# Moving three weight corrections from VectorE to GpSimd, and a reordered scatter queue, in a post-norm attention and mixture-of-experts layer

## Chip, cores, metric

The kernel runs on one core of a Trainium2 chip. The engines are TensorE (PE; its weight loads are PEld), VectorE (DVE), ScalarE (ACT), GpSimd (POOL) and SyncE (SP). The metric is device time in microseconds, lower is better.

## The reference

The input x is 2 x 2048 tokens of 256 channels. A linear attention adds a row to each token, a layer norm follows, then a mixture of 8 experts (2 chosen per token, hidden size 192) with a shared gated network, and a second layer norm.

```python
x = _layernorm(x + _L0_attn_ref(x, L0_attn_w_qkv, L0_attn_w_conv1), axis=-1)

def _L0_ffn_ref(x, gate_w, W1, W2, Ws1, Ws2):
    xf = x.reshape(-1, D)
    scores = jax.nn.softmax((xf @ gate_w.T).astype(jnp.float32), axis=-1)
    top_vals, top_idx = jax.lax.top_k(scores, K)
    w_dense = jnp.zeros((T, E), x.dtype).at[jnp.arange(T)[:, None], top_idx].set(weights)
    h = jnp.einsum('td,ehd->teh', xf, W1)
    y, g = jnp.split(h, 2, axis=-1)
    eo = jnp.einsum('teh,edh->ted', y * jax.nn.silu(g), W2)
    z = jnp.einsum('te,ted->td', w_dense, eo)
    z = z + _gated_mlp(xf, Ws1, Ws2)
    return z.reshape(x_shape)

x = _layernorm(x + _L0_ffn_ref(x, ...), axis=-1)
```

## The kernel before

All matmuls of the network run on numbers split into a high part and a low part (hi and lo, fp32r): lo = raw - hi. ACT writes the high parts, DVE or POOL subtracts for the low ones. The weights are split in ten pieces: `high(n)` on ACT (L686), `low(n)` on POOL (L550) for pieces 0 to 6, and `weights_lo(n)` on DVE (L1534) for pieces 7, 8 and 9. From piece 6 on, `low` cuts its work into instructions of 256 columns.

The 4096 tokens are 32 tiles of 128 (one token per partition), in eight groups of four. After the attention, the **group phase** handles groups 0 to 6 in a software pipeline. For each group g, DVE adds the attention row to the tiles (`layer_norm`, two groups ahead), ACT sums squares, POOL makes a rough reciprocal root (`rough_rstd`, L569), DVE refines it by one Newton step (`inverse_std`, one group ahead), ACT writes the normalised rows to x2 (`normalise`), TensorE transposes them (`transposes`), ACT and DVE split them (`rows_hi`, `rows_lo`), TensorE computes the router's logits and the shared network in three chunks of the hidden size (`first_layer`, `second_layer`), with silu on ACT and `product`, `hidden_lo` on DVE and `hidden_hi` on ACT between the layers. DVE picks the two experts of each token (`route`), keeps tables (`tables`) and computes each row's place (`slots`). POOL then scatters the group's rows to `rows_in` in HBM, eight indirect DMAs per group, two for each tile. x2 has two buffers: `normalise(g)` waits for the scatters of group g - 2 and for `add_routed_input` of group g - 2.

The **block phase** (`pairs`, L373) then runs the experts over 71 blocks of 128 rows in pairs, loads the rows from `rows_in`, and scatters the results; the last group's shared network and the second layer norm end it.

Each engine follows its own hand-written order; semaphores tie them. In POOL's loop over groups (L603 to L616) two tiles are scattered, then comes `rough_rstd(q + 2)`, then the other two; in group 6 and 7 a wait stands at that place instead, for the first half of `add_routed_input` of group 6 and for the first expert result. DVE's order in a group is `group(g)` (L1540); its first block is the router, its last `rows_lo` and `add_routed_input`.

## Time and profile before

| | |
|---|---|
| time, median of 3 runs | 334.84 us (333.88 to 335.81) |
| time of the profiled execution | 333.88 us |
| its span, first to last instruction | 332.1 us |
| PE busy | 307.7 us, 93% |
| DVE busy | 264.3 us, 80% |
| POOL busy | 197.2 us, 59% |
| ACT busy | 193.9 us, 58% |

The span is what the timelines count from. Groups 0 to 6 fill it from about 42 to 159 us, the block phase the rest. A row of a timeline gives the start, the duration, the engine, the line, the instruction as out<-in, a count, and in brackets how long the engine was idle before it and what ended that. Two neighbouring rows can overlap a little, since an instruction starts before the one ahead has drained. On PE an instruction's duration is longer than the distance to the next start.

### The profile page before, as it was taken

Reading aid. Unit: us, or ns where it says so; the run is one execution under the profiler, and the core shown is the slowest. Engines: PE = TensorE matmul, PEld = TensorE weight load, DVE = VectorE, ACT = ScalarE, POOL = GpSimd, SP = SyncE. Lnnn points to the kernel's source line nnn. Section 1 sums busy time; section 2 is a strip of 40 time slices with the busy share of each in tenths; the row PEclk is TensorE's granted clock in tenths of the full one; section 3 lists DMA queues with packets and bytes.
Section 4 is the critical chain, followed back from the end, with each engine's and each line's share of the span. In section 5 each row is a group of like instructions: output and inputs, shape, how many; then the busy total and the mean of one; then the engine's idle time right before and its main releaser. Section 6 shows DMA issues by size and latency. Waiting matters only on the chain.

```text
span 332.1 us, 7710 instructions
## 1 busy us (share of the span) xinstructions
PE 307.7 (93%) x2150; PEld 275.7 (83%) x2150; DVE 264.3 (80%) x1089; ACT 193.9 (58%) x440; POOL 197.2 (59%) x229
## 2 busy tenths in 40 slices
PE   3879899999999999999999999999999999999970
PEld 1446678789888889888999999999999999998770
DVE  1796889866888898865899877777799889987685
ACT  1044578846565554646356555666656588688473
POOL 5039580865784638465557544447676866777860
PEclk9979999999999999999999999999999999999977
DMA  6977331121292212442267544448998988976953
GB/s 210 393 270 243 108 92 36 69 100 49 70 254 70 75 42 98 121 147 84 82 200 244 181 131 137 141 125 201 253 211 199 246 203 205 246 214 178 333 193 126
DMA packets 31384, 54.63 MB, mean 164 GB/s; under 512 B 4881, under 2 KB 22545, under 8 KB 31345
## 3 DMA queue, kind: packets, MB, share of 16 engines
q1 hardware_dynamic: 23136, 29.82, 28.9%
q0 software_dynamic: 8208, 24.32, 26.1%
q8 instruction: 20, 0.33, 0.4%
q14 instruction: 20, 0.16, 0.2%
HBM read 29.73 MB, written 24.40 MB: 163 GB/s over the span
## 4 chain that ended last, share of the span: by engine, by line
PE 49%; DVE 18%; POOL 12%; DMA 7%; ACT 6%; issue 6%; SPq 1%; DVEq 0%; ACTq 0%; POOLq 0%
PE bank L1150 20%; PE bank L1184 11%; POOL rows_in L599 8%; PE bank L1116 4%; PE bank L901 4%; DMA rows_in<-x,slot 3%; ACT x L748 3%; DMA x<-rows_out 2%; POOL w1lo L556 2%; DVE mix L1493 2%; PE bank L1164 2%; DVE htlo L1499 2%; PE bank L1057 2%; POOL rough L577 2%; PE bank L1011 2%
## 5 line engine op out<-in xcount | busy, mean ns | idle before, releaser
L668 POOL DMA_INDIRECT rows_out<-stage,place x71 | 69.2, 974 | 46.4 <-ACT stage L847 32.7
L599 POOL DMA_INDIRECT rows_in<-x,slot x64 | 64.6, 1009 | 48.2 <-DVE slot L1405 27.7
L1150 PE MATMUL bank<-w1hi,bx 128*128 x284 | 64.0, 346 | 0.1
L1150 PEld LDWEIGHTS bank<-w1hi,bx 128*128 128x128 f32 x284 | 48.3, 188 | 0.6 <-issue 0.6
L827 ACT ACTIVATE stage<-bank 128x384 f32<-128x384 f32 (+1 forms) x36 | 17.5, 487 | 36.6 <-PE bank L1150 36.5
L847 ACT ACTIVATE stage<-bank,weight 128x256 f32<-128x256 f32 x71 | 30.0, 470 | 10.9 <-PE bank L1184 9.3
L1150 PE MATMUL bank<-w1lo,bx 128*128 x142 | 36.3, 336 | 0.0
L1514 DVE TENSOR_TENSOR bx<-bank,bx 128x512 fp32r<-128x512 f32 (+1 forms) x36 | 24.5, 684 | 13.5 <-ACT bx L768 13.1
L1057 PE MATMUL bank<-ws2hi,hthi 128*128 128x256 f32 x96 | 29.0, 302 | 3.3 <-DVE htlo L1499 3.3
L1033 PE MATMUL bank<-xthi,ws1hi 128*128 128x512 f32 x96 | 31.3, 407 | 0.6 <-DVE mix L1493 0.3
L1033 PE MATMUL bank<-xtlo,ws1hi 128*128 128x512 f32 x96 | 29.9, 393 | 0.0
L1033 PE MATMUL bank<-xthi,ws1lo 128*128 128x512 f32 x96 | 29.8, 392 | 0.0
L764 ACT ACTIVATE hthi<-mix 128x512 fp32r<-128x512 f32 x24 | 15.1, 629 | 23.5 <-DVE mix L1493 23.5
L760 ACT ACTIVATE mix<-bank 128x512 f32<-128x512 f32 x24 | 14.1, 588 | 23.3 <-PE bank L1033 23.2
L1057 PE MATMUL bank<-ws2hi,htlo 128*128 128x256 f32 x96 | 27.5, 286 | 0.0
L1057 PE MATMUL bank<-ws2lo,hthi 128*128 128x256 f32 x96 | 27.5, 286 | 0.0
L1150 PEld LDWEIGHTS bank<-w1lo,bx 128*128 128x128 f32 x142 | 25.7, 188 | 0.0
L1220 DVE CUSTOM_DVE_ANT_0 junk<-xs,bank 128x256 f32<-128x256 f32 x64 | 22.8, 415 | 3.2 <-DMA xs<-x 2.9
L1057 PEld LDWEIGHTS bank<-ws2hi,hthi 128*128 128x128 f32 x96 | 18.8, 196 | 5.7 <-issue 2.9
L1184 PE MATMUL bank<-w2hi,hthi 128*128 x71 | 22.8, 321 | 0.0
L1499 DVE TENSOR_TENSOR htlo<-mix,hthi 128x512 fp32r<-128x512 f32 x24 | 17.2, 716 | 6.7 <-ACT hthi L764 6.6
L768 ACT ACTIVATE bx<-bank 128x512 fp32r<-128x512 f32 (+1 forms) x36 | 21.2, 591 | 2.0 <-PE bank L1116 2.0
(255 smaller groups left out, 856.8 us busy)
## 6 DMA issues: line engine op xcount, KB each, us to landing
stage<-rows_in SPq DMA_DIRECT2D x71, 133.0 KB, 2.7
xs<-rows_out POOLq DMA_DIRECT2D x12, 512.0 KB, 6.1
xs<-x SPq DMA_DIRECT2D x8, 512.0 KB, 8.1
out<-xs SPq DMA_DIRECT2D x7, 512.0 KB, 5.3
stage<-w_t SPq DMA_DIRECT2D x8, 384.0 KB, 4.1
rows_in<-clear SPq DMA_DIRECT2D x16, 133.0 KB, 4.0
rows_out<-stage,place POOLq DMA_INDIRECT x71
stage<-w_t SPq DMA_DIRECT2D x2, 512.0 KB, 3.9
```

The costliest lines, as they stand in the source:

```text
L599: pool.indirect_dma_start(rows_in[0:E * CAP, :], bass.IndirectOffsetOnAxis(slot[:, q * G + t, k:k + 1], 0), x2[q % 2][:, t, :], None).then ...
L668: pool.indirect_dma_start(rows_out[:, :], bass.IndirectOffsetOnAxis(place[:, 2 * j + b:2 * j + b + 1], 0), by[j % 4][:, b * C:(b + 1) * C] ...
L768: act.activation(bxhi[j % 2][:, 0:C * width(j)], bank_x[j % 2][:, 0:C * width(j)], ACT.Copy).then_inc(s_bxhi, 1)
L827: act.activation(bsg[j % 2][:, 0:width(j)], bank_h[j % 2][:, 0:width(j), H:F], ACT.Silu).then_inc(s_bsg, 1)
L847: ins = act.activation(by[j % 4][:, b * C:(b + 1) * C], result(j, b), ACT.Copy, scale=weight[:, j // 2 % 2, at_w:at_w + 1])
L1033: mm = pe.matmul(bank[:], w[:, k, o:o + P], xt[:, k, :], start=(a == 0), stop=(a == len(steps) - 1))
L1057: mm = pe.matmul(bank[:, (t % 2) * C:(t % 2 + 1) * C], ht[:, m, t * P:(t + 1) * P], w[:, m, :], start=(t % 2 == 0 and n == 0 and a == 0), ...
L1150: mm = pe.matmul(bank_h[j % 2][:, b, 0:F], bx[j % 2][:, (2 * b + k) * P:(2 * b + k + 1) * P], w[:, bass.ds(e, 1), k, :], start=(a == 0), s ...
L1184: mm = pe.matmul(result(j, b), ht, w[:, bass.ds(e, 1), :], start=(a == 0), stop=(a == len(steps) - 1))
L1220: vec.tensor_tensor_reduce(junk[:, nth % 2, :], xs[:, tile, :], row, 1.0, 0.0, ALU.mult, ALU.add, dst[:, b, t:t + 1]).then_inc(s_dot, 1)
L1499: vec.tensor_tensor(htlo[:, c, :], prod[buf(g, m)], hthi[:, c, :].bitcast(F32), ALU.subtract).then_inc(s_ht, 1)
L1514: vec.tensor_tensor(bxlo[j % 2][:, at], bank_x[j % 2][:, at], bxhi[j % 2][:, at].bitcast(F32), ALU.subtract).then_inc(s_bx, 1)
```

## The change

POOL's loop over groups issues the eight scatters of a group in one row, with `rough_rstd(q + 2)` in their middle for groups 1 to 5 only; `rough_rstd(2)` follows the eight scatters of group 0. The two waits in groups 6 and 7 are dropped. After the scatters of groups 1 to 4 POOL does `low(6)` to `low(9)`; `weights_lo` is gone from DVE. On DVE in group 0, `token_shift(1)` and two tiles of `layer_norm(2)` come ahead of `rows_lo(1)`, the other two tiles behind it.

```diff
@@ POOL @@
-            def scatter(q, t):
-                for k in range(K):
-                    pool.indirect_dma_start(
...
             for q in range(NG):
                 pool.wait_ge(s_slot, q + 1)
-                for t in range(2):
-                    scatter(q, t)
-                if q < NG - 2:
-                    rough_rstd(q + 2)
-                elif q < LAST:
-                    pool.wait_ge(s_zev[0], q + 1)
-                else:
-                    pool.wait_ge(s_byev, results_signalled(1))
-                for t in range(2, G):
-                    scatter(q, t)
-                if q == 1:
-                    low(6)
+                for t in range(G):
+                    if t == 2 and 0 < q < NG - 2:
+                        rough_rstd(q + 2)
+                    for k in range(K):
+                        pool.indirect_dma_start(
...
+                if q == 0:
+                    rough_rstd(2)
+                elif q < 5:
+                    low(5 + q)
@@ DVE @@
-            def weights_lo(n):
-                vec.wait_ge(s_whi, n + 1)
-                vec.wait_ge(s_wlo, n)
-                vec.tensor_tensor(LO[n], RAW[n], HI[n].bitcast(F32), ALU.subtract).then_inc(s_wlo, 1)
-
             def group(g):
...
-                if 3 <= g <= 5:
-                    weights_lo(4 + g)
...
                 if g == 0:
                     hidden_lo(0, 2)
-                    rows_lo(1)
                     token_shift(1)
-                    layer_norm(after, range(G))
+                    layer_norm(after, range(0, 2))
                 if g > 1 and after < NG:
                     layer_norm(after, range(2, G))
                 if g:
                     hidden_lo(g, 2)
-                    rows_lo(g + 1)
+                rows_lo(g + 1)
+                if g == 0:
+                    layer_norm(after, range(2, G))
```

In the lists below, rough is the rough reciprocal root, vareps its input, rows_in the scattered rows, x_0 and x_1 the two buffers of normalised rows. POOL at group 0, before:

```order
L577 TENSOR_TENSOR rough<-vareps,half 128x4 [waits ln1_var_eps]
L599 DMA rows_in<-x_0,slot 33792x266 [waits slots,ln1_rstd]
L599 DMA rows_in<-x_0,slot 33792x266 x3
L575 TENSOR_SCALAR vareps<-square 128x4 [waits ln1_squares]
L577 TENSOR_TENSOR rough<-vareps,half 128x4 [waits ln1_var_eps]
L599 DMA rows_in<-x_0,slot 33792x266 x4
```

and now:

```order
L577 TENSOR_TENSOR rough<-vareps,half 128x4 [waits ln1_var_eps]
L602 DMA rows_in<-x_0,slot 33792x266 [waits slots,ln1_rstd]
L602 DMA rows_in<-x_0,slot 33792x266 x7
L575 TENSOR_SCALAR vareps<-square 128x4 [waits ln1_squares]
L577 TENSOR_TENSOR rough<-vareps,half 128x4 [waits ln1_var_eps]
L602 DMA rows_in<-x_1,slot 33792x266 [waits slots]
```

The rough root of group 2 has moved from behind four scatters to behind eight.

POOL from the end of group 2 to the start of group 4, before (w2lo and w2rlo are pieces 7 and 8):

```order
L599 DMA rows_in<-x_0,slot 33792x266 x4
L599 DMA rows_in<-x_1,slot 33792x266 [waits slots]
L599 DMA rows_in<-x_1,slot 33792x266 x3
L575 TENSOR_SCALAR vareps<-square 128x4 [waits ln1_squares]
L577 TENSOR_TENSOR rough<-vareps,half 128x4 [waits ln1_var_eps]
L599 DMA rows_in<-x_1,slot 33792x266 x4
L599 DMA rows_in<-x_0,slot 33792x266 [waits slots]
```

and now:

```order
L602 DMA rows_in<-x_0,slot 33792x266 x4
L556 TENSOR_TENSOR w2lo<-stage,w2hi 128x256 [waits weights_hi]
L556 TENSOR_TENSOR w2lo<-stage,w2hi 128x256 x3
L602 DMA rows_in<-x_1,slot 33792x266 [waits slots]
L602 DMA rows_in<-x_1,slot 33792x266 x3
L575 TENSOR_SCALAR vareps<-square 128x4 [waits ln1_squares]
L577 TENSOR_TENSOR rough<-vareps,half 128x4 [waits ln1_var_eps]
L602 DMA rows_in<-x_1,slot 33792x266 x4
L556 TENSOR_TENSOR w2rlo<-stage,w2rhi 128x256 [waits weights_hi]
L556 TENSOR_TENSOR w2rlo<-stage,w2rhi 128x256 x3
L602 DMA rows_in<-x_0,slot 33792x266 [waits slots]
```

Four pieces of a correction stand between the scatters of one group and the next.

DVE at the end of group 0, before (xtlo is `rows_lo`, small is `token_shift`, xs,rowsum is `layer_norm`, xs<-bank,x is `add_routed_input`):

```order
L1499 TENSOR_TENSOR htlo<-mix,hthi 128x512 [waits hidden_hi]
L1360 TENSOR_TENSOR xtlo<-bank,xthi 128x512 [waits x2t_hi] x2
L1262 COPY small<-bank 128x1 [waits att1_tensor]
L1280 SCALAR_TENSOR_TENSOR xs,rowsum<-row,tok,xs 128x256 x4
L1508 TENSOR_TENSOR xs<-bank,x_0 128x512 [waits shared_psum0]
L1508 TENSOR_TENSOR xs<-bank,x_0 128x512 [waits shared_psum1]
```

and now:

```order
L1491 TENSOR_TENSOR htlo<-mix,hthi 128x512 [waits hidden_hi]
L1254 COPY small<-bank 128x1 [waits att1_tensor]
L1272 SCALAR_TENSOR_TENSOR xs,rowsum<-row,tok,xs 128x256 x2
L1352 TENSOR_TENSOR xtlo<-bank,xthi 128x512 [waits x2t_hi] x2
L1272 SCALAR_TENSOR_TENSOR xs,rowsum<-row,tok,xs 128x256 x2
L1500 TENSOR_TENSOR xs<-bank,x_0 128x512 [waits shared_psum0]
L1500 TENSOR_TENSOR xs<-bank,x_0 128x512 [waits shared_psum1]
```

`rows_lo` has moved behind the small copy and two of the four tiles.

DVE in group 4 between the tables and the slots, before (mix is `product`, rn to minus is `inverse_std`, htlo is `hidden_lo`):

```order
L1471 SCALAR_TENSOR_TENSOR ends<-taken,ends 128x8 [waits table_steps]
L1538 TENSOR_TENSOR w2rlo<-stage,w2rhi 128x1024 [waits weights_lo,weights_hi,table_steps]
L1493 TENSOR_TENSOR mix<-bank,mix 128x512 [waits silu]
L1287 TENSOR_TENSOR rn<-rough 128x4 [waits ln1_newton0]
L1289 TENSOR_TENSOR rn<-vareps,rn 128x4 [waits ln1_newton1]
L1291 TENSOR_SCALAR rn<-rn 128x4 [waits ln1_newton2]
L1293 TENSOR_TENSOR rstd<-rough,rn 128x4 [waits ln1_newton3]
L1295 TENSOR_TENSOR minus<-nmean,rstd 128x4 [waits ln1_rstd]
L1499 TENSOR_TENSOR htlo<-mix,hthi 128x512 [waits hidden_hi]
L1493 TENSOR_TENSOR mix<-bank,mix 128x512 [waits silu]
L1280 SCALAR_TENSOR_TENSOR xs,rowsum<-att,tok,xs 128x256 x2
L1393 TENSOR_TENSOR slotf<-bank,begin 128x32 [waits positions]
```

and now:

```order
L1463 SCALAR_TENSOR_TENSOR ends<-taken,ends 128x8 [waits table_steps]
L1485 TENSOR_TENSOR mix<-bank,mix 128x512 [waits silu,table_steps]
L1279 TENSOR_TENSOR rn<-rough 128x4 [waits ln1_newton0]
L1281 TENSOR_TENSOR rn<-vareps,rn 128x4 [waits ln1_newton1]
L1283 TENSOR_SCALAR rn<-rn 128x4 [waits ln1_newton2]
L1285 TENSOR_TENSOR rstd<-rough,rn 128x4 [waits ln1_newton3]
L1287 TENSOR_TENSOR minus<-nmean,rstd 128x4 [waits ln1_rstd]
L1491 TENSOR_TENSOR htlo<-mix,hthi 128x512 [waits hidden_hi]
L1485 TENSOR_TENSOR mix<-bank,mix 128x512 [waits silu]
L1272 SCALAR_TENSOR_TENSOR xs,rowsum<-att,tok,xs 128x256 x2
L1385 TENSOR_TENSOR slotf<-bank,begin 128x32 [waits positions]
```

The correction of 1024 columns ahead of the product is gone, and the rest is as it was.

## Rows read from the trace of the kernel before

**Rows 1.** The page's costliest groups: busy, mean ns | idle before, releaser
```profile
L599 POOL DMA_INDIRECT rows_in<-x,slot x64 | 64.6, 1009 | 48.2 <-DVE slot L1405 27.7
```

**Rows 2.** Table of stretches: us, busy by engine, clock, DMA share, GB/s
```profile
105.00:122.00 17.00, 16.37 (x108) 14.20 (x106) 14.28 (x64) 9.30 (x24) 9.10 (x10) 1.00 0.18 65
...
sum 48.00, PE 47.01 PEld 41.13 DVE 41.72 ACT 25.67 POOL 27.94; mean PE 15.67 PEld 13.71 DVE 13.91 ACT 8.56 POOL 9.31
```

**Rows 3.** Timeline of PE: start, us, instruction, count [idle before, releaser]
```profile
60.84 0.71 PE L1033 MATMUL bank<-xthi,ws1hi 128*128 128x512 f32 x2 [0.18 <-DVE xs L1508]
...
73.85 1.09 PE L999 MATMUL bank<-ident,x 128*128 128x128 f32 x8
...
119.01 0.73 PE L1033 MATMUL bank<-xthi,ws1hi 128*128 128x512 f32 x2 [0.27 <-DVE mix L1493]
...
141.54 0.38 PE L1057 MATMUL bank<-ws2hi,hthi 128*128 128x256 f32 x1 [0.35 <-DVE htlo L1499]
```

**Rows 4.** Timeline of POOL, scatters of group 0
```profile
58.92 2.01 POOL L599 DMA_INDIRECT rows_in<-x,slot  x1 [0.30 <-issue]
...
62.50 0.96 POOL L599 DMA_INDIRECT rows_in<-x,slot  x1 [0.30 <-issue]
...
65.20 1.06 POOL L599 DMA_INDIRECT rows_in<-x,slot  x1 [0.20 <-issue]
...
69.10 0.96 POOL L599 DMA_INDIRECT rows_in<-x,slot  x1 [0.30 <-issue]
```

**Rows 5.** Timeline of DVE, groups 0 and 1
```profile
57.14 1.27 DVE L1360 TENSOR_TENSOR xtlo<-bank,xthi 128x512 fp32r<-128x512 f32 x2
...
66.51 0.15 DVE L1287 TENSOR_TENSOR rn<-rough 128x4 f32<-128x4 f32 x1
...
67.10 0.16 DVE L1293 TENSOR_TENSOR rstd<-rough,rn 128x4 f32<-128x4 f32 x1
...
69.56 0.69 DVE L1493 TENSOR_TENSOR mix<-bank,mix 128x512 f32<-128x512 f32 x1 [0.86 <-ACT mix L760]
```

**Rows 6.** Timeline of ACT, groups 1 and 5
```profile
70.29 0.63 ACT L764 ACTIVATE hthi<-mix 128x512 fp32r<-128x512 f32 x1 [0.76 <-DVE mix L1493]
71.72 2.08 ACT L748 ACTIVATE x<-xs,minus,rstd 128x256 f32<-128x256 f32 x4 [0.80 <-DMA rows_in<-x,slot]
...
136.15 2.08 ACT L748 ACTIVATE x<-xs,minus,rstd 128x256 f32<-128x256 f32 x4 [0.71 <-issue]
```

**Rows 7.** Line 1538, the corrections on DVE: ns min/median/max, first and last start
```profile
L1538 DVE TENSOR_TENSOR w2rlo<-stage,w2rhi x2: 1225/1250/1276, 117.1 to 132.5; 128x1024 fp32r<-128x1024 f32 x2
```

**Rows 8.** Timeline of POOL and DVE, group 2, around POOL's low(6)
```profile
85.11 0.63 DVE L1293 TENSOR_TENSOR rstd<-rough,rn 128x4 f32<-128x4 f32 x1
...
85.61 3.35 POOL L556 TENSOR_TENSOR w2lo<-stage,w2hi 128x256 fp32r<-128x256 f32 x4
...
85.78 0.66 DVE L1295 TENSOR_TENSOR minus<-nmean,rstd 128x4 f32<-128x4 f32 x1
...
86.36 1.31 DVE L1499 TENSOR_TENSOR htlo<-mix,hthi 128x512 fp32r<-128x512 f32 x1
...
88.19 1.06 DVE L1280 SCALAR_TENSOR_TENSOR xs<-att,tok,xs 128x256 f32<-128x256 f32 x1
...
89.18 0.47 DVE L1280 SCALAR_TENSOR_TENSOR xs<-att,tok,xs 128x256 f32<-128x256 f32 x1
```

**Rows 9.** Line 1499, htlo on DVE: ns min/median/max, first and last start
```profile
L1499 DVE TENSOR_TENSOR htlo<-mix,hthi x24: 659/690/1306, 51.3 to 320.2; 128x512 fp32r<-128x512 f32 x24
```

**Rows 10.** Timeline of POOL, scatters of groups 3 and 4
```profile
111.69 0.19 POOL L575 TENSOR_SCALAR vareps<-square 128x4 f32<-128x4 f32 x1 [1.04 <-ACT squares L723]
...
122.85 1.30 POOL L599 DMA_INDIRECT rows_in<-x,slot  x1 [4.79 <-DVE slot L1405]
...
133.57 0.96 POOL L599 DMA_INDIRECT rows_in<-x,slot  x1 [0.30 <-issue]
```

**Rows 11.** Timeline of POOL, scatters of groups 6 and 7
```profile
159.44 0.96 POOL L599 DMA_INDIRECT rows_in<-x,slot  x1 [1.83 <-DVE xs L1508]
...
173.26 0.96 POOL L599 DMA_INDIRECT rows_in<-x,slot  x1 [2.88 <-ACT stage L847]
```

More of the change, by code:

```diff
@@ L594, in _ @@
             pool.wait_ge(s_rs, 4)
-            def scatter(q, t):
-                for k in range(K):
-                    pool.indirect_dma_start(
-                        rows_in[0:E * CAP, :], bass.IndirectOffsetOnAxis(slot[:, q * G + t, k:k + 1], 0),
-                        x2[q % 2][:, t, :], None).then_inc(s_sc[q % 2], 16)
             for q in range(NG):
                 pool.wait_ge(s_slot, q + 1)
-                for t in range(2):
-                    scatter(q, t)
-                if q < NG - 2:
-                    rough_rstd(q + 2)
-                elif q < LAST:
-                    pool.wait_ge(s_zev[0], q + 1)
-                else:
-                    pool.wait_ge(s_byev, results_signalled(1))
-                for t in range(2, G):
-                    scatter(q, t)
-                if q == 1:
-                    low(6)
+                for t in range(G):
[3 more added lines that the diff above has]
+                        pool.indirect_dma_start(
+                            rows_in[0:E * CAP, :], bass.IndirectOffsetOnAxis(slot[:, q * G + t, k:k + 1], 0),
+                            x2[q % 2][:, t, :], None).then_inc(s_sc[q % 2], 16)
+                if q == 0:
+                    rough_rstd(2)
+                elif q < 5:
+                    low(5 + q)
             results = rows_out[0:DUMMY].rearrange("(k b p j) c -> k b p j c", k=K, b=B, p=P)
```

## The prediction

> **What bounds the kernel now.** I read the page's costliest groups first, then the table of stretches, then TensorE's own timeline for its waits, and last the timelines of POOL, DVE and ACT beside it. On the page POOL's scatters stand high, with 27.7 us of idling for DVE's slots ahead of them [rows 1]: POOL is waited for, but has room. In the group phase, where all the edits lie, TensorE is busy 47.01 of 48 us and DVE 41.72 [rows 2]. So the groups are TensorE's work laid end to end, and DVE, ACT and POOL matter only where a TensorE instruction waits for them. The reader should see in [rows 3] how small those waits are: 0.18 us for xs at the start of group 1, 0.27 us for the product in group 4, 0.35 us for htlo in group 5. What the edits can win there is no more than these waits. A delay has no such cap: an engine that is late by more than its slack pushes TensorE, and TensorE never catches up.
>
> **The change, part by part.** Durations are of one execution, whose time was 333.88 us (span 332.1, so 1.8 around it); the median of the three runs is 334.84, and I add the sum to the median.
>
> **1. rough_rstd(2) goes behind all eight scatters of group 0.** Before, it stands in the middle: a scatter ends at 62.50 + 0.96 = 63.46, the next one starts at 65.20, where otherwise 0.30 us lie between two, so the step costs the scatters 1.44 us. rough was ready at 65.00, the 0.20 before 65.20, and so 1.54 after that scatter. The last scatter ends at 69.10 + 0.96 = 70.06 [rows 4]. Now it ends at 70.06 - 1.44 = 68.62, and rough is ready not at 65.00 but at 68.62 + 1.54 = 70.16. Who waits? inverse_std(2) on DVE, which read rough at 66.51 with no wait [rows 5]: it now stands still 3.65 us. Queued behind it are value_row(1), two tiles of layer_norm(3), product(1, 1) and slots(1). From 66.51 to the start of DVE's idle 0.86 us before product(1, 1), that is to 68.70, is 2.19 us of work [rows 5], so the product starts at 70.16 + 2.19 = 72.35 instead of 69.56, 2.79 us late. ACT converts it (hthi, at 70.29 before, 0.73 after the product) and normalises group 2 behind that: at 72.35 + 0.73 + 0.53 = 73.61 instead of 71.72 [rows 6]. Until now ACT sat idle for 0.80 us before 71.72, for the scatters of group 0 to free the buffer; they are done 1.44 us sooner, which is the gain the move can have, but DVE is now later than they are. TensorE's transposes of group 2 started at 73.85, right behind the last of the four tiles [rows 3, 6]: they start **1.9 us later**, and everything after hangs on them. slots(1) is late too, 2.8 us, but the second half of those scatters waits for ACT's squares of group 3, which are 1.9 late as well.
>
> **2. rows_lo(1) goes behind two tiles of layer_norm(2).** It ran from 57.14 to 58.41 [rows 5], just before TensorE's logits of group 1. Two tiles at 0.47 at most [rows 8] and some 0.3 of waiting for TensorE's maximum (estimated from the order: it is issued behind second-layer matmuls) put its end at about 59.6, so the logits start 0.8 us late; the first-layer matmuls behind them waited for xs anyway, so 0.5 us is left at 60.84 [rows 3]. This delay lies inside the 1.9 us of part 1: with TensorE 0.5 us later, the chain through rough is still what ends last. It costs nothing by itself; if that cover were gone, it would cost 0.5.
>
> **3. Three corrections (w2lo, w2rlo) go from DVE to POOL.** DVE gives up 1.25 us in each of groups 3, 4 and 5 [rows 7]. POOL takes each as four pieces, behind the scatters of groups 2, 3 and 4. The one such set that POOL already does shows the price: four pieces in 3.35 us. POOL has that room: ahead of the scatters of group 4 it idled 4.79 us [rows 10], and 27.7 us over the eight groups [rows 1]. But DVE is slowed during it: rstd 0.63 where it took 0.16 in group 1 [rows 5], minus 0.66 for as short a step, htlo 1.31 where the median is 0.69, xs 1.06 where 0.47 [rows 8, 9], together 0.47 + 0.50 + 0.62 + 0.59 = 2.2 us. So DVE gives up 1.2 and may get back up to 2.2, and later in the group, right ahead of slots. The Trainium skill (SBUF — State Buffer, "two separate sides") says that DVE and GpSimd share a pair of ports under an exclusive lock, held for a whole instruction, and that a DVE instruction with two SBUF inputs is blocked by it. The rows agree: all four slowed ones read two tensors in SBUF. By that rule the move can lose on DVE what it was to gain.
> In groups 3 and 5 none of it reaches TensorE: the scatters that follow have 1.04 us of waiting for squares in their middle (one of two such rows in [rows 10]), and 0.7 us (three blocked instructions and a later start, less 1.2) fits in it. In group 4 two things happen. The product in front of which DVE did the correction comes 1.2 us sooner, and TensorE's wait of 0.27 goes. And slots(4) moves by -1.20 + (0.47 + 0.50 + 0.62) = +0.39, three of the four blocked instructions lying ahead of it. Its scatters run with no wait inside, 122.85 to the last start at 133.57 [rows 10], and normalise(6) on ACT starts 2.58 us after that, at 136.15 [rows 6]; behind it stands htlo, for which TensorE already waits 0.35 [rows 3]. So 0.39 goes through. The sum of group 4 is -0.27 + 0.39 = **+0.1**; its bounds are -0.27 - 0.35 = -0.6 with no slowing (more than the wait can't be won) and -0.27 + 0.98 = +0.7 with all four in front. I take +0.1, since the set in group 2 shows the slowing.
> The last correction is now ready behind the scatters of group 4, at 133.57 + 0.96 + 3.35 = 138; it is needed only by the blocks after group 6, whose xs was not ready before 159.4 [rows 11], so its place is free.
>
> **4. The waits of POOL in groups 6 and 7 go.** They cost POOL 1.83 and 2.88 us [rows 11]. Nobody waits for those scatters: there is no group 8 to normalise, and the rows they write are loaded for pair 8 and later. TensorE has no wait for POOL there. I take 0; against it stands only that the writes of group 7 now meet the loads of the first blocks' rows: +0.3 at most.
>
> The sum: 1.9 + 0 + 0.1 + 0 = **+2.0 us**, so 334.84 + 2.0 = **336.8 us**; the span would be 334.1.
>
> **The rivals.**
> **A: the second scatter gets shorter.** It took 2.01 us, where others take 0.96 [rows 4]; beside it four tiles of layer_norm, each at most 0.47, ran back to back on DVE from the end of rows_lo(1) at 58.4 to about 60. The change puts rows_lo, which reads PSUM, between them. If they were what held it, it takes some 1.05 now, and all of part 1 comes 0.95 earlier: +1.05, **335.9**. For it: the coincidence. Against it: tiles run beside the scatters of every group, and the longest of those later ones took 1.30 [rows 10]; the second may have been slow because it was one of the first. The same page of the Trainium skill names a trap in which DVE keeps GpSimd from writing its descriptors; it gives it for another kind of DVE instruction, so I leave this the smaller chance.
> **B: the slowing reaches TensorE in every group.** Then groups 3, 4 and 5 each pay 2.2 - 1.2 = 1.0 less the 0.27: +1.9 + 2.7 = +4.6 at worst, about half of it with the slack of 1.04 counted: +3.3, **338.1**. It decides from where a blocked instruction stands ahead of a TensorE wait with less slack than the block.
> **C: faster.** DVE, not TensorE, sets the pace of groups 3 to 5 (41.72 of 48 us busy), so the 3 x 1.25 = 3.75 us given up there come back in full and pay for part 1: 1.9 - 3.75 = -1.9, **333.0**. It decides once more than 3.6 of them reach TensorE. Against it: TensorE's waits there add up to under 1 us.
> **D: part 1 is covered.** TensorE does the second layer's first part before the transposes, and if POOL's rough is ready early enough (A) and group 4 wins its waits (-0.6), +0.3 is left: **335.1**, no change that can be told.
>
> **How the numbers follow.** Chances: forecast 0.52, A 0.17, B 0.12, C 0.07, D 0.12. A measurement of this kernel tells about 0.5% (1.7 us) from no change. The forecast lies 0.3 above that line; with its own spread (1.3 to 2.6) three quarters of it is over, so slower is 0.39 + 0.12 + a little of A = 0.53, faster 0.07, the rest 0.40. The range leaves out C and the worst of B: from 334.8 (D with 0.3 less) to 338.3 (B with 0.2 more).
>
> **What would show it.** Right: DVE idle for some 3.6 us ahead of rn in group 1 with POOL's rough as releaser; the transposes of group 2 near 75.8; DVE instructions over 0.6 us beside POOL's w2lo and w2rlo pieces in groups 3 to 5; the wait of 0.27 at 119 gone; the pairs of blocks at their present pace, the whole tail only shifted. Wrong: rough of group 2 ready by 68 (POOL faster than I think), a TensorE wait for a product or for htlo above 1 us in groups 3 to 5 (B), or slots that come earlier than before from group 4 on, in spite of a late group 2 (C).

## The result, and the profile after

The changed kernel took 337.4 us in the median of 20 runs, where the kernel before, run beside it, took 335.65: a ratio of 1.007 (95% interval 1.0051 to 1.009), or 2.35 us more. That is past the 0.5% that can be told, on the slower side, and inside the range; the forecast was +2.0. The profiled execution of the changed kernel took 340.0 us (span 338.3), among its slowest, while that of before (333.88) was among the fastest of its own. Their difference of 6.1 us is therefore more than the change, and durations of single steps are compared, not the two spans. One execution each of the kernel before, of e1 (350 us) and of e12 (517 us) ran at a low clock throughout (mean 0.84, 0.85 and 0.56), and the ratios and intervals below leave such executions out.

First the page of the changed kernel: busy time of each engine, the granted TensorE clock in 40 slices of the span (tenths of full speed), and the scatters with the idle time ahead of them.

```profile
PE 311.8 (92%) x2150; PEld 276.7 (82%) x2150; DVE 267.1 (79%) x1086; ACT 194.1 (57%) x440; POOL 204.7 (61%) x241
...
PEclk9959999699999999999999999999999999999996
...
L602 POOL DMA_INDIRECT rows_in<-x,slot x64 | 64.2, 1003 | 46.3 <-DVE slot L1397 29.7
```

The scatters are as before, with two us less of idling in all (46.3 against 48.2 in [rows 1]). New is the 6 in the eighth slice of PEclk, which is 59 to 68 us.

TensorE's timeline of the changed kernel; this answers [rows 3].

```profile
61.01 0.36 PE L1003 MATMUL bank<-gate,xthi 128*128 128x16 f32 x2 [0.77 <-DVE xtlo L1352]
...
63.30 1.20 PE L1025 MATMUL bank<-xthi,ws1hi 128*128 128x512 f32 x2
64.29 1.05 PE L1025 MATMUL bank<-xtlo,ws1hi 128*128 128x512 f32 x2
65.15 1.05 PE L1025 MATMUL bank<-xthi,ws1lo 128*128 128x512 f32 x2
...
78.63 0.60 PE L991 MATMUL bank<-ident,x 128*128 128x128 f32 x4
...
94.00 0.35 PE L1049 MATMUL bank<-ws2hi,hthi 128*128 128x256 f32 x1 [0.45 <-DVE mix L1485]
...
127.56 0.36 PE L1049 MATMUL bank<-ws2hi,hthi 128*128 128x256 f32 x1 [0.93 <-DVE mix L1485]
```

Three things differ. TensorE pauses for 0.77 us ahead of the logits of group 1, because rows_lo(1) now comes behind two tiles. Soon after, its pairs of first-layer matmuls start 0.86 us apart (64.29 to 65.15), where in the other trace they are about 0.46 apart. And in group 4 there is a wait of 0.93 us for a product, which before had no counterpart (the 0.27 us at 119.01 in [rows 3] is gone). The table of stretches of the changed kernel shows why the pairs are slow: us, busy time by engine, granted clock, DMA share and GB/s.

```profile
60.00:62.00 2.00, 1.23 (x12) 1.06 (x11) 2.00 (x7) 1.84 (x5) 1.52 (x2) 1.00 0.35 128
62.00:64.00 2.00, 2.00 (x11) 1.90 (x11) 1.24 (x5) 2.00 (x9) 1.46 (x2) 0.56 0.23 81
64.00:66.00 2.00, 2.00 (x6) 1.52 (x5) 1.85 (x20) 0.96 (x2) 1.62 (x2) 0.50 0.41 142
66.00:68.00 2.00, 2.00 (x6) 1.61 (x5) 0.38 (x2) 0.00 (x0) 1.39 (x3) 0.50 0.20 70
68.00:70.00 2.00, 2.00 (x26) 0.75 (x29) 0.57 (x1) 0.60 (x1) 1.84 (x3) 0.73 0.42 136
```

Behind the pause the granted clock was 0.50, the lower of TensorE's two levels (1.2 GHz), from about 62 to 69 us; from 62 to 70 us the mean is 0.57, so 8 x 0.43 = 3.4 us of full-speed work were lost. TensorE is "busy" all the time there, so the waits don't show it. This execution is not typical: its mean granted clock over the span is 0.970, where the median of the 45 recorded executions of the changed kernel is 0.981. The six of them at 0.973 or less took 338.8 to 340.1 us, the eight at 0.985 or more 335.3 to 337.4. The Trainium skill (TensorE: Matmul & The Clock Gate, "The HAM clock gate") has these two levels and says that idling brings the lower; here the level did fall behind a pause.

Now POOL, DVE and ACT of the changed kernel, for [rows 4] to [rows 6].

```profile
60.17 0.97 POOL L602 DMA_INDIRECT rows_in<-x,slot  x1 [0.31 <-issue]
...
67.86 0.96 POOL L602 DMA_INDIRECT rows_in<-x,slot  x1 [0.30 <-issue]
...
69.17 1.04 POOL L577 TENSOR_TENSOR rough<-vareps,half 128x4 f32<-128x4 f32 x1
...
69.43 0.69 DVE L1485 TENSOR_TENSOR mix<-bank,mix 128x512 f32<-128x512 f32 x1 [3.05 <-ACT mix L752]
...
71.42 0.15 DVE L1279 TENSOR_TENSOR rn<-rough 128x4 f32<-128x4 f32 x1
```

The eight scatters ran back to back, the second in 0.97 us instead of 2.01, and rough came at 70.21. DVE then read it at 71.42 without a wait. Its long idle stands earlier, 3.05 us ahead of product(1, 0): the late and slow TensorE had moved the wait to another place. The pause of 0.77 us is the only idle time of TensorE in this trace between 58 and 84 us.

Last, the price of POOL's pieces, for [rows 8]: POOL, DVE and ACT in groups 3 and 4 of the changed kernel.

```profile
107.25 2.84 POOL L556 TENSOR_TENSOR w2lo<-stage,w2hi 128x256 fp32r<-128x256 f32 x4
...
107.69 0.69 DVE L1485 TENSOR_TENSOR mix<-bank,mix 128x512 f32<-128x512 f32 x1 [0.43 <-ACT mix L752]
...
108.30 2.08 DVE L1272 SCALAR_TENSOR_TENSOR xs<-att,tok,xs 128x256 f32<-128x256 f32 x1
...
123.42 2.83 POOL L556 TENSOR_TENSOR w2rlo<-stage,w2rhi 128x256 fp32r<-128x256 f32 x4
...
122.89 0.66 DVE L1281 TENSOR_TENSOR rn<-vareps,rn 128x4 f32<-128x4 f32 x1
123.58 0.66 DVE L1283 TENSOR_SCALAR rn<-rn 128x4 f32<-128x4 f32 x1
124.28 0.65 DVE L1285 TENSOR_TENSOR rstd<-rough,rn 128x4 f32<-128x4 f32 x1
124.97 0.67 DVE L1287 TENSOR_TENSOR minus<-nmean,rstd 128x4 f32<-128x4 f32 x1
125.55 1.25 DVE L1491 TENSOR_TENSOR htlo<-mix,hthi 128x512 fp32r<-128x512 f32 x1
...
125.67 2.08 ACT L740 ACTIVATE x<-xs,minus,rstd 128x256 f32<-128x256 f32 x4 [1.73 <-DVE minus L1287]
```

In group 4 the pieces met the whole chain rn, rstd, minus: four steps of 0.16 us took 0.66 each, +2.0 us, and htlo another 0.6. (The first of the four, at 122.89, ended 0.13 us after the first piece began and stood beside the last scatter before that, so its 0.5 may belong to the scatter; in e3 it is the same.) ACT idled 1.73 us for minus. In group 3 they met one tile of layer_norm, which took 2.08 instead of 0.47.

### The profile page after: what moved, and what is told of

Its sections match the earlier page's. It is cut to its first block, busy times and chain, and to the rows that moved or that the text cites. A ratio compares the mean times of both kernels' runs of the same rounds, so it can differ in the third digit from the quotient of the medians.

```text
span 338.3 us, 7718 instructions
## 1 busy us (share of the span) xinstructions
PE 311.8 (92%) x2150; PEld 276.7 (82%) x2150; DVE 267.1 (79%) x1086; ACT 194.1 (57%) x440; POOL 204.7 (61%) x241
## 4 chain that ended last, share of the span: by engine, by line
PE 62%; DVE 22%; DMA 4%; issue 4%; ACT 4%; POOL 2%; SPq 1%; DVEq 0%; ACTq 0%
PE bank L1142 19%; PE bank L1176 10%; PE bank L1025 10%; PE bank L1049 4%; PE bank L1108 4%; PE bank L1003 4%; DVE xs L1272 3%; PE bank L893 3%; DVE htlo L1491 2%; DVE mix L1485 2%; DMA x<-rows_out 2%; POOL rows_in L602 2%; PE bank L1156 2%; PE bank L905 2%; DMA xs<-x 2%
## 5 line engine op out<-in xcount | busy, mean ns | idle before, releaser
L660 POOL DMA_INDIRECT rows_out<-stage,place x71 | 69.3, 977 | 48.0 <-ACT stage L839 34.2
L602 POOL DMA_INDIRECT rows_in<-x,slot x64 | 64.2, 1003 | 46.3 <-DVE slot L1397 29.7
L1025 PE MATMUL bank<-xthi,ws1hi 128*128 128x512 f32 x96 | 32.2, 417 | 0.2 <-ACT xthi L748 0.2
L1025 PE MATMUL bank<-xtlo,ws1hi 128*128 128x512 f32 x96 | 30.8, 403 | 0.0
L1025 PE MATMUL bank<-xthi,ws1lo 128*128 128x512 f32 x96 | 30.7, 401 | 0.0
L1049 PE MATMUL bank<-ws2lo,hthi 128*128 128x256 f32 x96 | 26.8, 279 | 0.0
L1049 PE MATMUL bank<-ws2hi,htlo 128*128 128x256 f32 x96 | 26.7, 279 | 0.0
L1049 PEld LDWEIGHTS bank<-ws2hi,hthi 128*128 128x128 f32 x96 | 18.1, 188 | 8.9 <-DVE htlo L1491 6.1
L1485 DVE TENSOR_TENSOR mix<-bank,mix 128x512 f32<-128x512 f32 x24 | 16.5, 686 | 8.6 <-ACT mix L752 8.5
```

The lines of the kernel that those rows point to most:

```text
L602: pool.indirect_dma_start(rows_in[0:E * CAP, :], bass.IndirectOffsetOnAxis(slot[:, q * G + t, k:k + 1], 0), x2[q % 2][:, t, :], None).then ...
L660: pool.indirect_dma_start(rows_out[:, :], bass.IndirectOffsetOnAxis(place[:, 2 * j + b:2 * j + b + 1], 0), by[j % 4][:, b * C:(b + 1) * C] ...
L1025: mm = pe.matmul(bank[:], w[:, k, o:o + P], xt[:, k, :], start=(a == 0), stop=(a == len(steps) - 1))
L1049: mm = pe.matmul(bank[:, (t % 2) * C:(t % 2 + 1) * C], ht[:, m, t * P:(t + 1) * P], w[:, m, :], start=(t % 2 == 0 and n == 0 and a == 0), ...
L1485: vec.tensor_tensor(prod[buf(g, m)], hidden_banks(g, m)[0][:], sg[buf(g, m)], ALU.mult).then_inc(s_pr, 1)
```

## The experiments

Two yardsticks are used. One is the time, measured beside the kernel before. The other is a span inside one profiled execution, from the start of the logits of one group to that of a later one; it leaves out how late the head of the kernel came. Starts are those of each kernel's first gate matmuls in the timeline of TensorE.

| kernel (us) | logits 0 to 1 | 1 to 2 | 0 to 2 | 4 to 5 | 5 to 6 | 2 to 7 |
|---|---|---|---|---|---|---|
| before | 15.15 | 19.66 | 34.81 | 16.30 | 16.02 | 81.46 |
| e4_waits | 15.15 | 19.54 | 34.69 | 16.17 | 17.84 | 83.19 |
| e1_rough | 15.14 | 21.39 | 36.53 | 16.15 | 17.82 | 83.09 |
| e2_rowslo | 16.10 | 19.09 | 35.19 | 16.17 | 17.81 | 83.34 |
| e11 (reorder again) | 16.10 | 18.97 | 35.07 | 16.19 | 17.83 | 83.64 |
| e3_lows | 15.16 | 19.56 | 34.72 | 17.36 | 16.30 | 83.38 |
| e5 (all but the reorder) | 15.14 | 21.40 | 36.54 | 17.46 | 16.19 | 83.40 |
| changed kernel | 16.10 | 22.09 | 38.19 | 17.38 | 16.19 | 83.36 |
| e9 (changed kernel again) | 16.08 | 21.09 | 37.17 | 17.36 | 16.37 | 83.71 |
| e10 (changed kernel, pause filled) | 16.00 | 22.11 | 38.11 | 17.34 | 16.28 | 83.32 |

The experiments e5 to e8 ran on a second chip and e9 to e12 on a third, where the kernel before took 348.7 and 346.8 us instead of 335.2. Ratios are only compared within a chip.

### One part alone: e1 to e4

**e1_rough**, only the move of rough_rstd(2):

```diff
-                if q < NG - 2:
+                if 0 < q < NG - 2:
                     rough_rstd(q + 2)
...
                 for t in range(2, G):
                     scatter(q, t)
+                if q == 0:
+                    rough_rstd(2)
```

> The kernel before with one edit: rough_rstd(2) stands behind all eight scatters of group 0. Theory P (the prediction, part 1): DVE stands still some 3.6 us ahead of rn in group 1, the transposes of group 2 start 1.9 us later (75.8 against 73.85 in the profile before), time +1.9 us. Theory Q (the trace of after, where rough came 68.6 to 70.2 and DVE had no wait for it, because TensorE itself was late): if the second scatter takes 0.97 again, rough is ready near 69 and the cost is about +1.0 us; it is hidden only if something else has delayed group 1.

It took 336.73 us (12 runs), ratio 1.0038 (1.0006 to 1.007), about +1.3. POOL, DVE and TensorE of e1_rough:

```profile
68.63 1.04 POOL L577 TENSOR_TENSOR rough<-vareps,half 128x4 f32<-128x4 f32 x1
...
69.70 0.16 DVE L1289 TENSOR_TENSOR rn<-rough 128x4 f32<-128x4 f32 x1 [3.54 <-POOL rough L577]
...
72.61 0.36 PE L1059 MATMUL bank<-ws2hi,hthi 128*128 128x256 f32 x1 [0.72 <-DVE mix L1495]
...
75.16 1.09 PE L1001 MATMUL bank<-ident,x 128*128 128x128 f32 x8 [0.94 <-ACT x L750]
```

That is the predicted mechanism to the tenth: DVE idle 3.54 us for rough (3.65 predicted), and TensorE waits 0.72 and 0.94 us. From the first layer at 60.40 to the transposes at 75.16 are 14.76 us, where [rows 3] give 13.01: +1.75, against +1.9 predicted. The table has +1.7 in group 1 and nothing in groups 0 and 4; the 17.82 in group 5 is explained under e4.

**e2_rowslo**, only the reorder around rows_lo(1):

```diff
-                    rows_lo(1)
                     token_shift(1)
-                    layer_norm(after, range(G))
+                    layer_norm(after, range(0, 2))
...
-                    rows_lo(g + 1)
+                rows_lo(g + 1)
+                if g == 0:
+                    layer_norm(after, range(2, G))
```

> The kernel before with one edit: rows_lo(1) stands behind token_shift(1) and two tiles of layer_norm(2). Theory P: TensorE's logits of group 1 start 0.8 us later, 0.5 us is left at the first layer, time +0.5 us. Theory R (the trace of after): the idle of 0.77 us ahead of the logits is followed by a stretch at the lower clock (granted 0.50 from 62.3 to 69), which costs over 3 us in that stretch: time +1.5 to +4 us, and the same dip in the profile of this run. If P holds the granted clock stays at 1.00 there.

It took 337.63 us (9 runs), ratio 1.0082 (1.0049 to 1.0116), about +2.7, as much as the whole change. Yet its profiled execution shows little. Its TensorE and POOL, then its table of stretches:

```profile
61.42 0.36 PE L1011 MATMUL bank<-gate,xthi 128*128 128x16 f32 x2 [0.77 <-DVE xtlo L1360]
...
60.55 0.97 POOL L599 DMA_INDIRECT rows_in<-x,slot  x1 [0.31 <-issue]
```

```profile
62.00:64.00 2.00, 2.00 (x17) 1.86 (x17) 1.75 (x9) 1.85 (x8) 1.70 (x2) 1.00 0.39 140
64.00:66.00 2.00, 2.00 (x10) 1.49 (x8) 1.86 (x18) 1.38 (x3) 1.41 (x3) 1.00 0.22 76
```

The pause of 0.77 us is there, the clock behind it is full this time, and the table gives +0.4 from logits 0 to 2: 0.95 lost in group 0, 0.5 won back in group 1. The other executions differ by their mean granted clock over the span: 0.979 in the median, against 0.985 for the kernel before. 0.006 of 335 us is 2 us of full-speed work. Its four executions at 0.983 or more took 336.0 to 337.4 us, its five at 0.979 or less 337.6 to 339.6. That pointed to the clock behind the pause, in some executions but not in the profiled one. It is not shown: the mean also covers the head (16 to 32 us) and the end (from 316 us on), where every trace of this chip has the lower level and loses 6.1 to 7.6 us in all, and no trace of this kernel has it behind the pause. It also shows that the second scatter is short (0.97) because of the reorder: in e1, e3 and e4, which leave the order alone, it took 2.01.

**e3_lows**, only the corrections moved to POOL:

```diff
-                if q == 1:
-                    low(6)
+                if 1 <= q <= 4:
+                    low(5 + q)
...
-                if 3 <= g <= 5:
-                    weights_lo(4 + g)
```

> The kernel before with one edit: pieces 7, 8 and 9 of the weight corrections on POOL behind the scatters of groups 2, 3 and 4, and not on DVE. Theory P: +0.1 us, TensorE's wait of 0.27 at group 4 gone, slots(4) 0.4 later. Theory B (slowing reaches TensorE): +1 to +3 us, with a TensorE wait of 0.9 in group 4 for the product, as the trace of after shows. Theory C (DVE was the pace): up to -3.7 us.

It took 335.67 us (12 runs), ratio 1.0026 (0.9999 to 1.0053), about +0.9. TensorE and ACT of e3_lows in group 4:

```profile
121.80 2.08 ACT L748 ACTIVATE x<-xs,minus,rstd 128x256 f32<-128x256 f32 x4 [1.70 <-DVE minus L1295]
...
123.70 0.36 PE L1057 MATMUL bank<-ws2hi,hthi 128*128 128x256 f32 x1 [0.92 <-DVE mix L1493]
```

The same two waits as in the changed kernel, without its other parts. Group 4 is 1.1 us longer in every kernel with this part (17.34 to 17.50) than in the others (16.15 to 16.60).

**e4_waits**, only the waits of POOL in groups 6 and 7 dropped:

```diff
                     rough_rstd(q + 2)
-                elif q < LAST:
-                    pool.wait_ge(s_zev[0], q + 1)
-                else:
-                    pool.wait_ge(s_byev, results_signalled(1))
```

> The kernel before with one edit: POOL's two waits in groups 6 and 7 are dropped. Theory P: 0 us, at most +0.3. Theory W (the waits kept descriptor work of POOL away from DVE and the loads at the start of the block phase): +0.5 us or more, with TensorE waits between 165 and 182 that the profile before does not have.

It took 334.88 us (12 runs), ratio 0.9996 (0.9964 to 1.0028): nothing, as predicted. It taught something else. Its group 5 took 17.84 us where before has 16.02, although the edit comes later in the program. ACT's normalise there:

```profile
138.75 2.07 ACT L744 ACTIVATE x<-xs,minus,rstd 128x256 f32<-128x256 f32 x4 [2.70 <-issue]
```

The idle of 2.70 was 0.71 in [rows 6]. Five traces have this late normalise (e1, e2, e4, e11, e12), and none of those with the corrections on POOL. What goes with it, without exception, is a race between DVE's correction w2rlo (the third of those that the change takes away) and one scatter of group 4. First DVE and POOL of e4, then of e7, which has the correction on DVE too:

```profile
133.08 1.23 DVE L1534 TENSOR_TENSOR w2rlo<-stage,w2rhi 128x1024 fp32r<-128x1024 f32 x1
...
133.28 1.86 POOL L599 DMA_INDIRECT rows_in<-x,slot  x1 [0.30 <-issue]
```

```profile
134.75 1.22 DVE L1541 TENSOR_TENSOR w2rlo<-stage,w2rhi 128x1024 fp32r<-128x1024 f32 x1
...
134.59 0.96 POOL L599 DMA_INDIRECT rows_in<-x,slot  x1 [0.30 <-issue]
```

In e4 DVE started 0.20 us ahead of the scatter, and the scatter took 1.86. In e7 the scatter started 0.16 ahead of DVE and took 0.96. So it is in all eight traces with this correction on DVE: DVE first by 0.20 or 0.21 in e1, e2, e4, e11 and e12 and the scatter 1.85 to 1.87 us long; the scatter first by 0.15 or 0.16 in before, e7 and e8 and 0.96 long. In the five, group 5 takes 17.81 to 17.84 us, 1.5 to 1.8 more than before's 16.02 or the 16.22 and 16.34 of e7 and e8. The delay has two halves. Counted from the logits of group 5, the last scatter of group 4 starts 0.9 to 1.0 us later, and from its start to the normalise it is 3.3 us, where the three that won the race have 2.6 to 2.9; why it lands later is not settled. The corrections on POOL end this race. They cost 1.1 us in group 4 each time and save up to 1.7 in group 5 in those executions that lose it; that this is why e3 pays only 0.9 in all is argued and not shown, since how often the kernel before loses the race was not measured. The trace of before was one that won it, so the prediction could not see a gain there.

The four parts measured +1.3, +2.7, +0.9 and -0.1, together +4.8, against +2.35 (1.7 to 3.0) for the whole. Each part is known to about 1 us and their sum to about 2, so that the parts overlap is likely and not certain. The next runs asked where.

### The pause and the clock: e5 to e8

**e5_after_old_rows**, the changed kernel with the old order around rows_lo(1):

```diff
+                    rows_lo(1)
                     token_shift(1)
-                    layer_norm(after, range(0, 2))
+                    layer_norm(after, range(G))
...
-                rows_lo(g + 1)
-                if g == 0:
-                    layer_norm(after, range(2, G))
+                    rows_lo(g + 1)
```

> The changed kernel with rows_lo(1) put back ahead of token_shift(1) and the whole of layer_norm(2): parts 1, 3 and 4 of the change without part 2. Theory A (costs add up): rough_rstd(2) alone measured +1.3 us and the low pieces +0.9 us, so this gives about +2.2 us, 337.4, as much as the whole change, with VectorE idle some 3 us ahead of rn in group 1 and the transposes of group 2 about 1.7 us later after the first layer than in before. Theory B (the reorder is the dear part, because TensorE's 0.8 us pause ahead of the logits of group 1 is followed in many executions by a granted clock of 0.5, while the wait of part 1 is then hidden): the time lies below that of the changed kernel only if A's two costs are smaller than what the reorder costs; the mean granted clock over the span returns to about 0.985 from the changed kernel's 0.981, and no slice between 60 and 70 us is granted less than 1.00.

352.42 us (6 runs), ratio 1.0104 (1.007 to 1.0138), +3.6 on this chip, more than e1 and e3 together on the first (+2.2). The clock was 1.00 from 60 to 80 us, and DVE's wait for rough is back:

```profile
71.46 0.16 DVE L1279 TENSOR_TENSOR rn<-rough 128x4 f32<-128x4 f32 x1 [3.55 <-POOL rough L577]
```

Up to the logits of group 7 the costs add as Theory A says (36.54 and 17.46 in the table are e1's and e3's numbers). The rest of the +3.6 lies behind group 7: from those logits to the last matmul it took 177.8 us, and 173.7 in e7 and e8 on the same chip. On the first chip the changed kernel took 162.2 there and the kernel before 162.7.

**e6_after_filled**, the changed kernel with work in the pause:

```diff
                     pe.wait_ge(s_slot, g)
+                if g == 1:
+                    for _ in range(14):
+                        pe.matmul(banks[2][:, 256:384], onesb[:], onesb[:], start=True, stop=True)
                 pe.wait_ge(s_xt, g + 1)
```

> The changed kernel with 14 more matmuls of 128 columns (bf16 ones into an unused part of bank 2) between TensorE's two waits ahead of the logits of group 1, about 0.8 us of work where it paused for 0.77 us. They are not part of the computation. Theory B (the pause itself is cheap, the clock behind it is dear): the granted clock stays 1.00 from 60 to 72 us, the mean clock goes from 0.981 to about 0.985 and the time falls by 1 to 1.5 us, to 336.0 to 336.4; the wait of part 1 then shows itself again. Theory A (contention and waits alone, the clock plays no part): the extra matmuls change nothing or cost up to 0.5 us, 337.4 to 337.9.

**e7_reorder_filled**, e2 with the same addition:

> The kernel before with the reorder alone (rows_lo(1) behind two of the four tiles of layer_norm(2)) and the same 14 matmuls in TensorE's pause ahead of the logits of group 1. The reorder alone measured +2.7 us. Theory B (clock): most of this goes, +0.8 or less is left, which is what the late low parts of the rows take from TensorE: 335.2 to 336.0, mean clock 0.985. Theory A (the order on VectorE makes work late by itself): +2.7 us stays, 337.9, and the mean clock says nothing.

**e8_head_filled**, the kernel before with such matmuls in the head:

```diff
+            pe.wait_ge(s_set, 1)
+            warm(6, banks[6])
             channel_logits(0)
+            warm(18, banks[6])
             token_column(0)
+            warm(8, banks[6])
             token_row(0)
```

(and six more inside channel_logits(0).)

> The kernel before with 38 matmuls of 128 columns (bf16 ones into bank 6, before its first use) in four pauses of TensorE between 13.5 and 19.5 us (0.52, 0.52, 1.44 and 0.58 us long in the trace of before); they are not part of the computation. In every profile so far the granted clock is about 0.5 for 3 to 4 us somewhere between 20 and 32 us. Theory B (a pause brings it): with the pauses filled the clock stays 1.00 there, TensorE wins up to 1.5 us of the head, and as much as the head's later waits let through reaches the end, 0 to -1.5 us: 333.7 to 335.2. Theory C (it comes with the rise of work at 20 us, whatever the pauses were): the low clock stays, and the time is that of before or up to 0.3 us more.

e6 took 355.33 us (6 runs), ratio 1.0207 (1.0167 to 1.0247); e7 348.59 (12 runs), 1.0001 (0.9972 to 1.0029); e8 349.25 (12 runs), 1.0009 (0.9979 to 1.0039). e7 fits Theory B, e6 speaks against it, and neither had its unfilled partner on that chip; e9 to e12 mend this. e8 is a miss. Its clock was full where before had the low level (0.57 from 20 to 24 us), but it fell later, behind the next pause. Its table of stretches, and below it one line of e2's:

```profile
20.00:24.00 4.00, 4.00 (x60) 2.87 (x59) 3.79 (x23) 2.32 (x3) 1.65 (x1) 1.00 0.80 271
24.00:28.00 4.00, 2.60 (x37) 2.01 (x35) 3.83 (x24) 1.48 (x1) 4.00 (x4) 1.00 0.27 78
28.00:32.00 4.00, 3.98 (x41) 1.77 (x38) 1.09 (x7) 1.99 (x4) 3.77 (x3) 0.58 0.95 316
```

```profile
28.00:32.00 4.00, 4.00 (x43) 2.01 (x40) 1.17 (x7) 1.99 (x4) 3.71 (x3) 0.57 0.93 316
```

The shift can't be put down to the filling. e2 and e11, whose head is that of the kernel before, also have the clock at 1.00 from 20 to 28 us and at 0.57 from 28 to 32; the other eleven traces have the low level between 16 and 26. So the place of this stretch changes between executions of the same head.

### Filled and unfilled on one chip: e9 to e12

e9 is the changed kernel, e10 is e6, e11 is e2 and e12 is e7, word for word.

> The changed kernel itself, beside its filled version on one chip. It was 0.7% slower than before (interval 1.0051 to 1.009) where the kernel before takes 335.6 us. The chip of the last four experiments took 348.7 us for the kernel before and had a 3 us wait at the routing of the last group that no trace of the first chip shows, so ratios of the two chips are not to be mixed. Both theories: 1.005 to 1.009 on a chip like the first; on one like the second Theory A (low pieces and first-scatter wait add up: e5 measured 1.0104 there without the reorder) gives 1.010 to 1.015.

> The changed kernel with 14 extra matmuls in TensorE's pause ahead of the logits of group 1, now beside the changed kernel on the same chip. Theory B (the low clock behind the pause is what the reorder costs): the clock is 1.00 from 60 to 72 us, and the kernel is 1 to 1.5 us faster than e9. Theory A' (with the clock full, TensorE only meets the late rn of part 1 sooner and waits there, as a 1.7 us pause between 66 and 72 us in the second chip's trace suggests): within 0.5 us of e9.

> The kernel before with the reorder alone, beside its filled version on one chip. It measured 1.0082 (1.0049 to 1.0116) on the first chip, with a mean clock of 0.979 against 0.985. Both theories: 1.005 to 1.011 again on a chip like the first. If it is 1.002 or less, the +2.7 us of the first measurement was an accident of its nine runs and the reorder is cheap, as the prediction had it.

> The reorder alone with the 14 extra matmuls in the pause. It measured 1.0001 (0.9972 to 1.0029) on the second chip, where the unfilled version was not run. Theory B: 1.0 to 1.002, thus 1.5 to 2.5 us faster than e11, with a mean clock 0.004 to 0.006 higher. Theory A (late work on VectorE, no part for the clock): equal to e11 within 0.5 us.

| kernel | median us (runs) | ratio to before | 95% interval | median clock |
|---|---|---|---|---|
| e9, changed kernel | 353.23 (6) | 1.0177 | 1.0135 to 1.0218 | 0.970 |
| e10, the same, filled | 352.64 (6) | 1.0179 | 1.0143 to 1.0216 | 0.974 |
| e11, reorder alone | 348.04 (12) | 1.0039 | 1.0002 to 1.0076 | 0.976 |
| e12, the same, filled | 347.12 (12) | 1.0019 | 0.9989 to 1.0049 | 0.978 |

With the pause filled the clock stayed at 1.00 from 60 to 72 us in all four traces, but the changed kernel is not faster: e9 and e10 are equal in time, as Theory A' had it, though not for its reason (below). In the reorder alone filling gains 0.9 us of the 1.4; the intervals overlap, and it is less than the 1.5 to 2.5 that was expected, so this has the sign of Theory B and doesn't prove it. Two more expectations missed: e9's 1.0177 lies above both bands, and e11's 1.0039 below its own. The tables of stretches of e9 (first two lines) and of e10 (last two), and below them what TensorE and ACT of e10 did:

```profile
64.00:66.00 2.00, 2.00 (x6) 1.60 (x5) 1.69 (x14) 0.79 (x1) 1.70 (x2) 0.50 0.42 144
66.00:68.00 2.00, 2.00 (x19) 0.92 (x22) 0.14 (x1) 0.60 (x1) 1.39 (x3) 0.73 0.23 83
```

```profile
64.00:66.00 2.00, 2.00 (x25) 1.14 (x27) 1.85 (x18) 0.21 (x1) 1.39 (x3) 1.00 0.22 76
66.00:68.00 2.00, 0.99 (x13) 0.44 (x6) 0.51 (x4) 0.00 (x0) 1.70 (x2) 1.00 0.41 136
```

```profile
64.90 2.00 PE L893 MATMUL bank<-xs,stage 128*32 128x256 f32 x27
67.90 0.43 PE L893 MATMUL bank<-xs,stage 128*32 128x256 f32 x2 [1.00 <-issue]
...
69.37 0.60 ACT L752 ACTIVATE mix<-bank 128x512 f32<-128x512 f32 x1 [5.17 <-remote]
```

e9 has the low clock again behind its pause. e10 has none, but both TensorE and ACT stood still until 69.3 us for reasons that the profile doesn't name: TensorE in the middle of 32 matmuls between which the program has no wait. e6, on another chip, has the same stop at the same place (0.19, 0.34 and 0.99 us, and 5.30 for ACT). e7 has none from 60 to 72 us, nor has e12, though TensorE's program is the same; what differs there is POOL, which in e6 and e10 issues its eight scatters without a step between them. That alone doesn't bring the stop either: POOL does the same in the changed kernel, e9 and e5, where TensorE stands still without a named reason for at most 0.50 us from 60 to 72 us. So in e10's trace filling removed one loss and another stood in its place. What stopped the two engines stays open.

Behind group 7 the slower chips differ in two more ways. e9's TensorE at the routing of the last group, and a stretch of its table:

```profile
172.92 0.21 PE L1034 MATMUL bank<-chosen,trib 128*128 128x40 bf16 x1 [3.18 <-DVE chosen L1379]
```

```profile
188.00:190.00 2.00, 1.69 (x8) 1.73 (x9) 1.80 (x11) 1.62 (x4) 0.96 (x1) 0.50 0.73 181
```

The wait for DVE is 3.0 to 3.4 us long in all four traces of the changed kernel and its variants there (e5, e6, e9, e10) and in e7, and absent in e8, e11, e12 and on the first chip. The low clock comes between 168 and 194 us in all eight traces of e5 to e12, costs 1.7 to 5.1 us of full-speed work, and comes in none of the first chip. It takes 3.4 us more in e5 than in e8 and 1.7 more than in e7, a good part of the 4.1 us by which e5 is longer behind group 7. No run changed either of the two alone.

## Why the prediction was right, point by point

- **What bounds the kernel.** Right: where TensorE's idle or its clock differs, the span differs; DVE's and POOL's own totals don't tell it.
- **1, rough_rstd(2), +1.9.** Right, and shown alone: +1.75 in e1's trace, +1.7 in group 1 in e1 and e5, +1.3 (0.2 to 2.3) in time. In the changed kernel the wait itself is not seen: rough was ready at 70.21 and read at 71.42, because TensorE was late already. So of the signs that the prediction named, its first one (DVE idle 3.6 us for rough) is absent there, and the transposes of group 2 came at 78.63 us and not near 75.8, of which 1.2 is a later head.
- **2, rows_lo(1), 0 under the cover of part 1.** This step failed. The 0.8 of late logits was right (0.93 to 0.95 in the traces with the reorder, 0.84 to 0.87 with the pause filled), and so was the 0.5 left without cover (+0.4 from logits 0 to 2). But the cover did not hold: with both parts (the changed kernel, e6, e9, e10), logits 0 to 2 took 37.17 to 38.41, which is 2.4 to 3.6 more than before's 34.81 and not 1.9. In the changed kernel's trace it was the other way round, the lost clock hid the wait of part 1; in e6 and e10 the unexplained stop stood there. And the price of a pause was taken to be its length. Behind it the granted clock fell to 0.50, for some 7 and 3 us, in both traces of the changed kernel (there and in e9), in neither trace of the reorder alone (e2, e11), and in none of the ten traces without the pause was it under 1.00 from 60 to 72 us. By those rows a pause of 0.77 us cost 3.4 us more in one execution and 1.7 in another (e9, from 62 to 68 us). In the median it was less: the mean clock is 0.981 against 0.985 for the kernel before (beside e1 to e4), 1.3 us of full-speed work, wherever in the span it was lost.
- **3, the corrections, +0.1.** The contention was right and mis-sized. The prediction took three blocked instructions and their effect on slots; it was the chain rn, rstd, minus with htlo behind it, 2.0 + 0.6 us, and it reached TensorE by way of ACT's normalise and the product (waits of 0.92 in e3, 0.93 in the changed kernel). Group 4 paid 1.1, above the bound of +0.7. What the step left out altogether is the gain in group 5, up to 1.7, of a scatter that no correction of DVE can meet. In time the part cost +0.9 (0 to 1.8).
- **4, the dropped waits, 0.** Right (e4).
- **The rivals.** A's premise was true: the second scatter takes 0.97 once the order changes, shown by e2. Its price of -0.95 did not come, since that scatter was no longer what ended last. B was true in one group out of three. C is refused: taking 3.75 us from DVE won nothing (e3). D did not happen.

So the sum of 2.0 met the 2.35 partly by luck, by errors that cancel. Between the traces of e4 and of the changed kernel, logits 0 to 2 differ by 3.5 us instead of 1.9, group 4 by 1.2 instead of 0.1, and group 5 by -1.65 instead of 0. The shares in the medians are not settled more finely than the intervals of e1 to e4 allow.

## What to carry to other kernels

A pause on an engine that never catches up costs its length and may cost more: after moving work past a wait of TensorE, read the granted clock in the stretch behind it, because an engine at half clock is shown as busy. Before handing work to POOL, look for what runs beside it on DVE, and which scatters it frees: a chain of tiny steps can be hit once by each piece, so that in group 4 four steps of 0.16 us took 2.0 us more. And don't let one delay "cover" another until you have shown that both end at the same wait.

## What the runs showed of the hardware

- One POOL instruction of 128x256 (0.74 us) holds up DVE steps that meet it and read only SBUF: 0.66 us instead of 0.16 for 128x4, 1.25 instead of 0.69 for htlo. The product (mix, at 107.69 in the changed kernel), which has one of its inputs in PSUM, took its usual 0.69 beside a piece. The holding up was seen for a TENSOR_SCALAR with one tensor too, not only for steps with two tensors. One DVE step of 0.47 took 2.08, longer than two pieces: it didn't get its turn when the first piece ended. The Trainium skill (SBUF — State Buffer, "two separate sides") has the lock and names both kinds of DVE step, where the prediction had read the rows as if two tensors were needed.
- Whether DVE or POOL comes first decides who is held up: a scatter that starts 0.15 us before a 1.23 us correction of DVE takes 0.96 us, one that starts 0.20 after it takes 1.86. The same page says that whichever starts first has the pair for its whole instruction; the eight traces agree at this place. They don't at the correction of group 4, where in six traces (before, e1, e2, e4, e11, e12) DVE started 0.01 to 0.03 us ahead and the scatter still took 0.96 us, DVE's step 1.27 to 1.29 instead of 1.23. The first group's scatter of 2.01 (0.96 or 0.97 in every trace with a step that reads PSUM between the tiles of layer_norm) looks like the same thing. Such a race can go either way in executions of one program (e7 won it and e12, the same kernel on another chip, lost it), and it moved group 5 by 1.5 to 1.8 us.
- The low clock came behind a pause of 0.77 us in two executions and not in two others: 0.50 in the changed kernel and e9, 1.00 in e2 and e11, which have the reorder alone. Whether the rest of the change decides this or the execution does, four traces can't tell; e2 and e11 are also the ones whose low stretch in the head came late (28 to 32 us).
- Chips differ more than the change: the kernel before took 335.2, 348.7 and 346.8 us on three of them. In the traces of the two slower ones TensorE idles with no releaser named ("issue") for 0.8 to 4.8 us in the block phase, with or without the change (e5 to e12), and not at all on the first chip. The change itself costs more there, 1.8% (1.35 to 2.2) against 0.7%. Most of the rest lies behind group 7, and its cause is open apart from the two things named under e9 to e12.
- No version was faster than the kernel before; e4, at 0.9996, is equal to it.
